# Context and weights transposed by the host's layout instead of by TensorE, and one unrolled list of steps per engine

## What is computed

```python
def attn(x):                       # stream A, x = layernorm(x)
    q, k, v = x @ w_q, x @ w_k, x @ w_v
    A = softmax(q @ k.T / sqrt(128))
    return ((A @ v) * head_dim_mask) @ w_o

def xattn(x, y, y_mask, W, b):     # stream B, y is the context
    x_proj = relu(x @ W.T + b)
    y_proj = relu(y @ W.T + b)
    scores = where(y_mask, -inf, x_proj @ y_proj.T)
    return softmax(scores) @ y

def ffn(x):                        # stream C; act_quant to 8 bits, weight_quant to -1, 0, 1 times a mean
    gate = silu(bitlinear(x, w_gate)); up = bitlinear(x, w_up)
    return bitlinear(gate * up, w_down)

x = x + attn(ln(x)); x = x + xattn(ln(x), ctx, mask, W, b); x = x + ffn(ln(x))
```

## Time and profile before

| | |
|---|---|
| median of three runs | 442.1 us (440.67 to 443.67) |
| span of the profiled execution | 440.3 us |
| PE busy | 405.4 us (92%) |
| DVE, ACT, POOL busy | 352.1, 348.5, 237.2 us |
| DMA, mean over the span | 39 GB/s, 17.36 MB |
| mean granted TensorE clock | 0.981 |

### The profile page before, as it was taken

The page is one execution under the profiler, slowest core; times in us unless marked ns, Lnnn a source line. Parts: engine busy times, 40 slices in busy tenths (PEclk is TensorE's granted clock), DMA queues, the critical chain, the costliest instruction groups (busy, mean ns, idle before and its releaser), DMA issues.

```text
span 440.3 us, 8582 instructions
## 1 busy us (share of the span) xinstructions
PE 405.4 (92%) x2585; PEld 319.0 (72%) x2614; DVE 352.1 (80%) x929; ACT 348.5 (79%) x651; POOL 237.2 (54%) x298
## 2 busy tenths in 40 slices
PE   3969999999999999999999999999999996997865
PEld 3847788767886788768876788768876785676533
DVE  2987368769988898879996999789996978598673
ACT  3359997987797978997899789988898876767571
POOL 2015802565458634675547645683657644657672
PEclk9999999999999999999999999999999998899888
DMA  7853100010001010001100101010100110001011
GB/s 242 311 169 115 50 0 1 0 49 1 2 1 48 1 48 2 2 0 49 49 0 0 48 11 38 0 48 0 48 0 0 48 48 0 0 1 48 1 44 53
DMA packets 16890, 17.36 MB, mean 39 GB/s; under 512 B 992, under 2 KB 16480, under 8 KB 16864
## 3 DMA queue, kind: packets, MB, share of 16 engines
q1 hardware_dynamic: 16864, 17.04, 11.7%
HBM read 12.85 MB, written 4.19 MB: 39 GB/s over the span
## 4 chain that ended last, share of the span: by engine, by line
PE 76%; ACT 8%; DVE 7%; POOL 3%; issue 3%; DMA 1%; POOLq 0%; SPq 0%; DVEq 0%; ACTq 0%
PE b_bank L683 9%; PE b_bank L685 9%; PE b_bank L684 9%; PE a_bank L683 6%; PE d_bank L852 6%; PE a_bank L685 5%; PE a_bank L684 5%; PE g_bank L836 5%; PE u_bank L836 5%; PE a_bank L737 3%; PE b_bank L792 3%; PE t_bank L844 3%; PE b_bank L766 2%; PE u_bank L689 2%; POOL c_work L479 2%
## 5 line engine op out<-in xcount | busy, mean ns | idle before, releaser
L479 POOL TENSOR_TENSOR c_work<-c_work 128x512 f32<-128x512 f32 x64 | 81.9, 1286 | 52.3 <-ACT c_work L612 36.8
L1008 DVE SCALAR_TENSOR_TENSOR c_work<-c_work,g_bank 128x512 f32<-128x512 f32 x56 | 38.1, 681 | 17.9 <-ACT c_work L609 17.9
L609 ACT ACTIVATE c_work<-g_bank,c_tanh_scale 128x512 f32<-128x512 f32 x56 | 38.6, 690 | 13.5 <-PE g_bank L836 9.6
L494 POOL TENSOR_SCALAR c_work<-c_work,h_q 128x1024 f32<-128x1024 f32 x32 | 36.1, 1129 | 9.2 <-DVE h_q L1029 9.2
L618 ACT ACTIVATE h_T<-t_bank 128x1024 bf16<-128x1024 f16 x32 | 32.9, 1028 | 9.2 <-PE t_bank L844 9.2
L1020 DVE TENSOR_REDUCE h_max<-c_work 128x1 f32<-128x1024 f32 x32 | 38.7, 1210 | 0.9 <-POOL c_work L479 0.8
L683 PE MATMUL b_bank<-ctx_hi,b_pT_hi 128*128 128x256 f32 x128 | 39.3, 307 | 0.0
L852 PE MATMUL d_bank<-downT,h_T 128*128 128x256 bf16 x256 | 36.2, 288 | 0.8 <-DVE x_all L1013 0.7
L612 ACT ACTIVATE c_work<-u_bank 128x512 f32<-128x512 f32 x56 | 33.6, 600 | 4.1 <-PE u_bank L836 3.9
L685 PE MATMUL b_bank<-ctx_hi,b_pT_lo 128*128 128x256 f32 x128 | 36.1, 282 | 0.0
L684 PE MATMUL b_bank<-ctx_lo,b_pT_hi 128*128 128x256 f32 x128 | 36.1, 282 | 0.0
(11 more groups left out here) (188 smaller groups left out, 1325.0 us busy)
## 6 DMA issues: line engine op xcount, KB each, us to landing
x_all<-in_x SPq DMA_DIRECT2D x8, 512.0 KB, 3.4
ctx_raw<-in_ctx SPq DMA_DIRECT2D x8, 512.0 KB, 3.3
out<-x_all SPq DMA_DIRECT2D x7, 512.0 KB, 3.0
c_work<-in_L_ffn_w_gate SPq DMA_DIRECT2D x1, 1024.0 KB, 8.2
c_work<-in_L_ffn_w_up SPq DMA_DIRECT2D x1, 1024.0 KB, 10.6
c_x<-in_L_ffn_w_down SPq DMA_DIRECT2D x1, 1024.0 KB, 5.3
mask_u<-in_mask_BxS_bk SPq DMA_DIRECT2D x1, 512.0 KB, 7.0
out<-x_all SPq DMA_DIRECT2D x4, 128.0 KB, 1.7
```

Of the source, the lines that this page charges most:

```text
L479: pool.tensor_tensor(h[:, t % 2, half * HALF:(half + 1) * HALF], th[:, j % 2, :], up[:, j % 2, :], ALU.mult).then_inc(hs, 1)
L494: pool.tensor_scalar(h[:, t % 2, :], h[:, t % 2, :], h_q[:, t:t + 1], ROUND_F16, ALU.mult, ALU.add).then_inc(hqs, 1)
L609: act.activation(th[:, j % 2, :], gu_bank("g", j, n), ACT.Tanh, scale=c_tanh_scale[:, t:t + 1]).then_inc(tanhs, 1)
L1008: dve.scalar_tensor_tensor(th[:, j % 2, :], th[:, j % 2, :], 1.0, gu_bank("g", j, n), ALU.add, ALU.mult).then_inc(gates, 1)
```

## The change

1. The host transposes. The launch now gets the context twice, once by tokens (ctx) and once transposed (ctx_t), W, w_gate, w_up and w_down transposed, q, k and v weights stacked, and x and out with all rows of a partition next to each other. CT0 and CT1 fall away; YP reads ctxT_hi and ctxT_lo, which ACT (`round_ctxT`) and POOL (`ctxT_rest`) form from the loaded ctxT_raw. prep_T and its evictions fall away: ACT's sign writes gateT, upT and downT directly.
2. x_all has five slots in place of eight. x/5, x/6 and x/7 are loaded in the list of SP, each after the store of three batches' distance has completed.
3. Every engine has one full list (*_ORDER), no loop. The small extra instructions of the loop form (`carry`) are gone.
4. The lists are newly ordered.

The core of the diff:

```diff
-B_STEPS = ["CT0", "CT1", "YP0", "YP1", "XT0", "XT1", "XP0", "XP1", "S0", "S1",
+B_STEPS = ["YP0", "YP1", "XT0", "XT1", "XP0", "XP1", "S0", "S1",
...
+X_SLOTS = 5
+
+PE_ORDER = """
+    B.YP0/0 A.XT0/0 A.XT1/0 B.YP1/0 A.V/0 A.Q/0 A.K/0 A.VT/0 A.S0/0 A.S1/0 A.P0/0 A.S2/0 A.P1/0 A.S3/0 W.total/0
...
+ACT_ORDER = """
+    B.ctxT/0 W.hi/0 B.ctx/0 A.norm/0 B.mask/0 B.YP0/0 A.XT0/0 A.XT1/0 B.YP1/0 A.norm/1 A.V/0 A.Q/0 A.K/0 A.VT/0
+    B.ctxT/1 A.exp0/0 A.exp1/0 A.P0/0 A.exp2/0 A.P1/0 A.exp3/0 A.P2/0 A.P3/0 W.sign0/0 W.sign1/0 A.H/0 W.sign2/0
+    W.sign3/0 W.sign4/0 W.sign5/0 A.XT0/1 A.XT1/1 A.norm/2 B.norm/0 A.V/1 A.Q/1 B.XT0/0 B.XT1/0 A.K/1 A.VT/1
...
+SP_ORDER = """
+    S.ctx/1 S.ctxT/1 S.ctxT/2 S.ctx/2 S.ctxT/3 S.ctx/3 S.ctxT/4 S.store/0 S.ctx/4 S.x/5 S.ctxT/5 S.store/1
...
         def x_tile(n, t):
-            if isinstance(n, int):
-                return x_all[:, n, t, :]
-            return x_all[:, bass.ds(n, 1), t, :].rearrange("p o d -> p (o d)")
+            return x_all[:, n % X_SLOTS, t, :]
...
             def load_x(n):
...
+                if n >= X_SLOTS:
+                    sp.wait_ge(out_stored, 16 * (n - X_SLOTS + 1))
+                sp.dma_start(x_all[:, n % X_SLOTS], x[:, n]).then_inc(x_loaded, 16)
...
+            def load_ctxT(n):
+                if n > 0:
+                    sp.wait_ge(ctxT_loaded, n * 16)
+                    sp.wait_ge(ctxT_split, n)
+                sp.dma_start(ctxT_raw[:, :, :], ctx_t[:, n]).then_inc(ctxT_loaded, 16)
...
             load_x(0)
-            sp.dma_start(W_raw, W.rearrange("(c p) d -> p c d", p=P)).then_inc(W_loaded, 16)
...
+            sp.dma_start(wqkv_raw, w_qkv).then_inc(qkvo_loaded, 16)
+            sp.dma_start(W_raw, W.rearrange("p c d -> p (c d)")).then_inc(W_loaded, 16)
+            load_ctxT(0)
+            sp.dma_start(bias[:, :], b).then_inc(W_loaded, 16)
+            sp.dma_start(wo_raw, w_o).then_inc(qkvo_loaded, 16)
+            sp.dma_start(hm_i[:, :], head_mask).then_inc(qkvo_loaded, 16)
             load_ctx(0)
...
             for j, w in enumerate((w_gate, w_up, w_down)):
-                if j == 2:
-                    sp.wait_ge(qkvo_split, 1)
...
+                sp.dma_start(ffn_raw[j], w.rearrange("p c d -> p (c d)")).then_inc(ffn_loaded[j], 16)
             load_x(1)
             sp.dma_start(mask_u8[:, :, :], mask[:, :].partition_broadcast(P)).then_inc(mask_loaded, 16)
-            for n in range(2, B):
+            for n in range(2, X_SLOTS):
                 load_x(n)
...
+            def ctxT_rest(n):
+                pool.wait_ge(ctxT_his, n + 1)
+                pool.tensor_tensor(ctxT_lo[:, :, :], ctxT_raw[:, :, :], f32(ctxT_hi[:, :, :]), ALU.subtract).then_inc(ctxT_split, 1)
...
+                act.activation(ffn_dst[j][:, half], ffn_raw[j][:, half], ACT.Sign, bias=neg_round[:, :]).then_inc(w_ternary, 1)
+
+            def round_ctxT(n):
+                act.wait_ge(ctxT_loaded, 16 * n + 16)
+                if n > 0:
+                    act.wait_ge(ctxT_split, n)
+                    act.wait_ge(b_filled, NB * (n - 1) + 2)
+                act.activation(ctxT_hi[:, :, :], ctxT_raw[:, :, :], ACT.Copy).then_inc(ctxT_his, 1)
...
-                if step[:2] == "CT":
...
-                    for s in range(T):
-                        mm = pe.transpose(dst[:, s * P:(s + 1) * P], ctx_raw[:, s, t * P:(t + 1) * P], ident[:, :])
...
+                    if step[0] == "Y":
+                        if n == 0 and t == 0:
+                            pe.wait_ge(W_split, 1)
+                        pe.wait_ge(ctxT_split, n + 1)
+                        if n > 0:
+                            pe.wait_ge(b_added, T * n - 1 + t)
+                        hi, lo = ctxT_hi, ctxT_lo
...
-            with pe.Fori(FIRST_FULL, B) as i:
-                run(PE_LOOP, step, i)
-            run(PE_LAST, step)
+            run(PE_ORDER, step)
...
+        "ctx": tokens(ctx),
+        "ctx_t": ctx.reshape(*ctx.shape[:2], -1, P).transpose(3, 0, 2, 1),
...
+        "W": rows(inputs["L0_xattn_W"].T),
```

## The result

The changed kernel is slower: 458.3 us (median of 4 runs, 456.4 to 460.0) against 441.4 us of the kernel before (4 runs, 440.0 to 443.7) on the same chip. The ratio is 1.039, with a 95% interval of 1.034 to 1.043. The forecast was 440.9 with a range up to 449. The profiled execution of the changed kernel has a span of 454.6 us, which stands against the 439.1 of my sum.

The account below looks back on a forecast made before the run. TensorE (PE) was taken as the bound in the dense part; five stages, 55.8 + 76.0 + 225.3 + 51.5 + 30.5, sum to 439.1 us, plus 1.8 for the median gives 440.9, with an 8-in-10 range of 430 to 449.

Parts of the forecast that it names:

- What bounds the kernel, the price of PE's steps: Dense part: PE is the bound, busy 235.33 of 236.90 us, so a removed step saves the time it occupied.
- stage 3: V/3 to the end of A.Y1/7: shorter by 11.6 us, to 225.3, from removed CT steps and moved C work.
- POOL then has 31.6 of about 47.3 us, so in the steady part it hides behind PE: Steady batches: POOL gains ctxT_lo, 2.39 us per batch, claimed hidden behind PE.
- Rival 3: Gaps in the steady part, 1 us in each of five batches: 446 us; chance 0.1.
- The wait for b_xn is now covered ... so I allow 5.4 lost instead of 11.8: Ramp-down before XQ/7: ten us of C/4, C/5 and B/6 work would cover PE's b_xn wait.
- stage 4: End of A.Y1/7 to XQ/7: 46.1 us of PE work plus 5.4 lost, 51.5 us, longer by 6.5.
- stage 5: XQ/7 to the end: C/7 alone plus HT2, DN1 and DN2 of C/6, 30.5 us, longer by 0.6.
- Rival 2: Ramp-down goes at C's own pace, 89.1 us instead of 82.0 after A.Y1/7, total 448.0; chance 0.16.
- B/7 runs beside C/5 and fills PE: Ramp-down: the argument that another stream's work would keep PE filled, against C's own pace setting the length.
- Stage 1: Up to V/1: later by 12.5 us, to 55.8, held by the x/1 load on DVE and ctxT/1 on ACT.
- Stage 2: V/1 to V/3: shorter by 9.2 us, to 76.0, being 71.2 of PE work plus 4.8 for waits.
- The removed work: Per batch, CT0 and CT1 leave PE, saving 0.87 us; unrolling the loop priced at 0 to 0.9.

Follow-up runs that it names:

- p_split4: Changed kernel with GpSimd's ctxT_lo as four instructions of 256 columns in place of one of 1024; 455.8 us.
- t_splice: p_split4 with the steps from A.V/7 on in the order of the kernel before, so less of C is left at the end; 471.5 us.
- s_start: p_split4 with the start reordered: mask, x/1 statistics, weight sums and other steps the first batch does not need moved later on ACT, DVE, POOL; 461.3 us.
- c_columns: Changed kernel, ctxT_lo whole, with c_clip and c_q on DVE as four 128x1 instructions each instead of one 128x4; 451.2 us.
- t_two_banks: p_split4 with gate and up steps 3, 5 and 7 of batch 5 writing the two free banks of stream A; 453.0 us.
- o4_places: Host layout and written-out lists in the old order, ctxT_lo in four instructions, ctxT steps re-placed on ACT and POOL; 435.1 us, ratio 0.984 to the kernel before.
- u_before: Kernel before with only its loop over batches 4 to 7 written out on all engines, same order; 438.8 us.
- after: The changed kernel itself, with all edits of the change, against the kernel before; 458.3 us.
- q_on_dve: p_split4 with the rounding of h (hq) of batches 5, 6 and 7 on DVE instead of POOL; 463.2 us.

## Why the prediction was wrong

- **What bounds the kernel, the price of PE's steps: right.** With the collision on DVE taken out, stage 3 is 225.0 to 225.4 us in eight kernels, 225.3 forecast, and the iteration 47.2, 47.3 forecast.
- **"POOL then has 31.6 of about 47.3 us, so in the steady part it hides behind PE": wrong, the step that failed in the middle.** Its time is hidden from PE's queue but not from DVE: the 2.4 us held c_q for 2.10, q_lo was queued behind it, and A.VT on PE waited for q_lo. I had asked only whether POOL has room. That is 1.4 us per batch and, by p_split4, 5.0 of the +5.1 in stage 3. Rival 3 had the size (1 us per batch) and POOL's 2.39 in its list, at a chance of 0.1, but not the way it acts.
- **"The wait for b_xn is now covered ... so I allow 5.4 lost instead of 11.8": wrong, the step that failed at the end, and the largest.** I took 82.0 us for stages 4 and 5; they took 91.6. The 11.8 is the length of stage 4 before, less the price of its steps. The wait of 4.1 us for b_xn did go, but other waits took its place: the same difference is now 56.1 - 46.1 = 10.0, not 5.4, with PE idle for 6.8 us where it was 7.5. So the 12.9 us of work put into stage 4 made it 11.1 longer and not 6.5. In stage 5 I had +0.6; the steps that the list has there on top (DN1/6, HT2/6) are 1.3 by my own prices, and it took 5.6 more, 3.8 of it busy PE, at clock 0.79 instead of 0.87. Over both stages PE's idle time went from 18.3 to 19.4 us: the added work filled no gaps. How the 16.7 divides between C's pace and the clock the runs do not show, only that holding up the clock with extra products does not give it back.
- **Rival 2, C's own pace, was near in its number** (89.1, at a chance of 0.16), and my argument against it, "B/7 runs beside C/5 and fills PE", did not hold. That C alone goes slower than its PE price is shown (26.6 us for 11.0 in t_splice). That this pace is what sets the whole ramp-down is not: there the added work cost 1.2 times its price.
- **Stage 1: the number right, the reason one of three.** V/0 was forecast at 24.3 by x/1, landing at 19.8 (the terms add up to 24.2); it landed by 19.34, and V/0 was at 24.3, the difference being DVE's wait for ACT behind the mask. That the number came out to a tenth is luck. The Trainium skill's fit, page "DMA: Bandwidth & Descriptors", section on the anatomy of one DMA, is given there for one DMA on the GpSimd path. Taken for this queue of ten on SyncE, it gave 16.5; the trace has 19.34. But with x/1 and the mask out of the way the YP steps and warm-up on PE still held V/0 at 24.1 (s_start), and ACT stood at the mask until 20.59, so x/1 alone was not the cause. ACT had ctxT/1 at 32.4, not 34.8, and exp0/0 came at 33.4, not 36, so stage 1 was 3.4 us shorter, in a profile that also kept the clock; most others of the new order had V/1 at 55 to 57, around my 55.8, by a lower clock that I had not priced.
- **Stage 2: +4.2 us, open.** One part is the same collision (c_clip 2.13 us at 93.5, PE waits 2.0 for q_lo), but p_split4 and c_columns still need 80.8 to 81.0 and t_two_banks 79.8. The allowance of 4.8 us for waits was too small. In p_split4 PE's longest waits there are for DVE's low parts in stream A (2.2 us for a_xT_lo, 1.9 for k_lo, 1.5 for a_pT_lo), where o4_places has none over 1.4; I ran nothing that takes them apart.
- **The removed work: right in sign, less in size.** The CT steps were to give 0.87 us per batch; o4_places against u_before shows 0.6 (47.2 against 47.8). Writing out the loop gave 0.4 per iteration, 1.6 over the four and 2.7 in the median, more than the 0 to 0.9 that I had for the whole kernel.
- **The chances.** I gave slower by over 1% 0.19. Terms of the size of rivals 2 and 3 both came in at once, each a term of its own on top of the same sum; 448.0 + 5.1 is nearer to what happened than any single case I priced. I treated them as alternatives where they add.

## What to carry to other kernels

Before giving an idle engine a long instruction, look at what runs beside it on the engines that share something with it: GpSimd's 2.4 us were free for GpSimd and cost 1.4 us per batch through a 128x4 operation on VectorE; split the long instruction or write the short one in a form that does not collide. In a software pipeline, do not count on the gaps of the ramp-down to take in work that a new order leaves for it: here 14.2 us of steps made it 16.7 longer, though PE idled 18.3 there, and a dependent chain caught up nearly alone took 26.6 for 11.0. So compare how much of each stream is left when the last batch of the first one ends. At a start, take all covers away before you judge one: here mask, x/1 and two early steps of another stream covered one another.

## What the runs showed of the hardware

- A one-input VectorE operation of 128x4 took 2.10 us while GpSimd ran a 2.4 us instruction, ending within 0.03 us of it; of 128x1 four took 0.34 us under it, and a RECIPROCAL of 128x4 0.18 (after, c_columns). A 128x1024 one took 1.85 instead of 0.75 us beside GpSimd's 1.26 (q_on_dve).
- With the same lists the granted clock in the thin chain of the first batch stayed at 1.00 in two profiles and was 0.83 to 0.89 on average in four, 0.60 in the 8 us of p_split4 shown above; 27 extra products held it at 1.00, with V/1 3 us earlier (53.2 against 56.2).
- With the loop (62 steps on PE) written out on all engines, an iteration took 47.8 us instead of 48.2.
